# Eight row buffers and a new clearing in a Flamingo kernel's first feed-forward stage, and a second stage that routes a pair of blocks ahead

## The reference

```python
# layer 0: shared expert of width 8*128 plus 8 routed experts of width 4*128, two per token, each expert takes at
# most CAPACITY = 1.25 * 3200 / 8 = 500 tokens; the rest are dropped for it
y = (silu(x @ sg) * (x @ su)) @ sd
p = softmax(rms(x) @ router_w.T); top 2 of 8; weights p_k / (p_1 + p_2)
y += sum_k weight_k * (silu(x @ rg[e_k]) * (x @ ru[e_k])) @ rd[e_k]      # where the token's place in e_k < CAPACITY
# layer 1: shared expert of width 128 plus 32 routed experts of width 64, four per token
p = softmax(x @ gw + gb)
group score = sum of the best 2 of each group of 4 experts; keep the 4 best of 8 groups; top 4 experts of the kept
y = shared(x) + sum_k p_k * expert_k(x)                                    # silu(x@w1+b1) * (x@w3+b3) @ w2 + b2
```

## Time and profile before

| | us |
|---|---|
| median of 3 runs (lowest, highest) | 6456.21 (6451.88, 6462.94) |
| the profiled execution's own time | 6469.54 |
| its span, first to last instruction | 6467.7 |
| first feed-forward stage, from and to | 1387.3, 1811.2 |
| of it the 64 dense tiles, from | 1403.4 |
| of it the 32 expert tiles, from | 1610.8 |
| second feed-forward stage, from and to | 3624.9, 4134.9 |
| third feed-forward stage (unchanged), about, from and to | 4530, 4950 |

### The profile page before, as it was taken

How to read it: one execution, slowest core, us unless ns; L and a number is a source line. 1 busy time by engine, 2 the same in 40 slices (tenths; PEclk the granted TensorE clock), 3 DMA queues, 4 the chain that set the end, 5 groups by cost and what they waited for, 6 DMA issues and landing times. The chain is left out here.

```text
span 6467.7 us, 117098 instructions
## 1 busy us (share of the span) xinstructions
PE 5589.6 (86%) x40832; PEld 3686.0 (57%) x40832; DVE 4453.7 (69%) x12146; ACT 3253.6 (50%) x4807; POOL 1778.2 (27%) x1263
## 2 busy tenths in 40 slices
PE   6999999978559999999999566687496999999996
PEld 4666666647435555555555355455496566665663
DVE  6777777756356666666666577544676877788775
ACT  3666666644324444444444343333354566666664
POOL 2222222204122222222222023344364222222220
PEclk9999999988769999999999778788798999999998
DMA  3333333321133333333332133266232332333320
GB/s 78 74 72 73 74 74 74 75 63 34 38 94 78 78 78 78 78 78 78 77 76 66 42 64 62 68 192 170 91 111 81 74 73 66 71 70 75 74 61 22
DMA packets 220512, 494.21 MB, mean 76 GB/s; under 512 B 35531, under 2 KB 154242, under 8 KB 219773
## 3 DMA queue, kind: packets, MB, share of 16 engines
q1 hardware_dynamic: 214341, 483.03, 30.8%
q0 software_dynamic: 5632, 4.23, 0.3%
HBM read 262.45 MB, written 12.97 MB: 43 GB/s over the span
## 5 line engine op out<-in xcount | busy, mean ns | idle before, releaser
L850 PE MATMUL a_max<-a_stack,a_qblk 96*100 96x482 f32 (+1 forms) x4608 | 2003.3, 455 | 115.5 <-DVE a_mx L671 35.9
L550 ACT ACTIVATE a_probs<-a_scores 128x800 f32<-128x800 f32 (+1 forms) x1536 | 1281.5, 838 | 1019.9 <-PE a_scores L867 657.0
L863 PE MATMUL a_scores<-a_qblk,a_stack 128*128 128x400 f32 (+1 forms) x4608 | 1379.1, 372 | 5.9 <-POOL a_qblk L455 2.9
L665 DVE CUSTOM_DVE_ANT_0 a_dump<-a_max,a_mqf 100x482 f32<-100x482 f32 (+1 forms) x1536 | 978.7, 657 | 426.6 <-PE a_max L850 395.4
L850 PEld LDWEIGHTS a_max<-a_stack,a_qblk 96*100 96x100 f32 x4608 | 767.5, 167 | 746.6 <-issue 207.2
L671 DVE CUSTOM_DVE_ANT_0 a_dump<-a_max,a_penq 100x482 f32<-100x482 f32 (+1 forms) x1536 | 956.3, 657 | 274.0 <-PE a_max L850 252.5
L657 DVE TENSOR_REDUCE a_mx<-a_max 100x1 f32<-100x482 f32 (+1 forms) x1536 | 941.9, 655 | 260.1 <-PE a_max L850 242.3
L879 PE MATMUL a_pv<-a_probs,a_v_aug 128*32 128x200 f32 x18432 | 1052.1, 340 | 3.4 <-ACT a_probs L548 2.1
L863 PEld LDWEIGHTS a_scores<-a_qblk,a_stack 128*128 128x128 f32 (+1 forms) x4608 | 840.3, 186 | 181.6 <-issue 52.6
L548 ACT ACTIVATE a_probs<-a_scores,a_kbias 128x800 f32<-128x800 f32 (+1 forms) x768 | 697.6, 926 | 409.4 <-PE a_scores L863 409.1
L431 POOL TENSOR_TENSOR a_klo<-a_kf,a_khi 128x1444 fp32r<-128x1444 f32 x96 | 316.4, 3296 | 1507.8 <-ACT a_khi L511 1062.9
(11 more groups left out here) (390 smaller groups left out, 7314.5 us busy)
## 6 DMA issues: line engine op xcount, KB each, us to landing
a_stack<-a_khi SPq DMA_DIRECT2D x768, 180.5 KB, 3.4
a_ctxT<-in_ctxT_dram SPq DMA_DIRECT2D x128, 722.0 KB, 8.3
a_stack<-a_klo SPq DMA_DIRECT2D x384, 180.5 KB, 3.6
f_wb<-weights_by_token SPq DMA_DIRECT2D x16, 1600.0 KB
f_wb<-weights_by_token SPq DMA_DIRECT2D x64, 400.0 KB
a_ctxn<-in_ctxn_dram SPq DMA_DIRECT2D x32, 704.0 KB
a_mt_i<-in_mask1T_dram SPq DMA_DIRECT2D x32, 600.0 KB, 6.9
a_mq_i<-in_mask_dram SPq DMA_DIRECT2D x32, 564.1 KB
```

Of the source, the lines that this page charges most:

```text
L550: act.activation(out_, in_, ACT.Exp, scale=scale).then_inc(sc_free, 1)
L665: nc.vector.tensor_tensor_reduce(dump[:, k % 2, 0:n], src, mqf[:, b % 2, o:o + n], 1.0, -3.0e38, ALU.mult, ALU.max, out_).then_inc(mx_free, 1)
L850: pe.matmul(to[0:S, 0:n], qblk[0:96, b % 2, HALF * h + head, :], stack[0:96, b % 2, g, o:o + n], start=True, stop=True).then_inc(mx_full, 1)
L863: ins = pe.matmul(out_, stack[:, b % 2, 2 * h + g, kt * D:kt * D + r], qblk[:, b % 2, HALF * h + 4 * g:HALF * h + 4 * g + 4, :].rearrange( ...
```

## The change

In the first stage `got` has eight buffers instead of three, and SP issues all eight row fetches one after the other as soon as the scatters have landed, ahead of the weight parts of experts 3 to 7. `rows_by_slot` is cleared from 80 partitions (50 rows each, 528 B pieces as before), `rows_by_token` in pieces of 1024 floats (4 KB) out of a zeroed stretch at the end of `rows`. POOL's number fills of `sent` and DVE's normalising of the last block wait for the clearing, since they write there.

The second stage gets a function of its own, `grouped_ffn_phase`, without a hardware loop. The routing is made for two blocks at a time and one pair ahead, all x splits of the 8 blocks have buffers, group and expert choice use DVE's max and match_replace instructions, and the weight parts come in a new order.

```diff
-    LOADS = 2
+    BLANKS = 80
...
-        blank = sb("blank", [SLOT, ROW])
-        zero = sb("zero", [S, D])
-        got = sb("got", [SLOT, 3, 4, ROW])
+        blank = sb("blank", [BLANKS, ROW])
+        zero = rows[:, (B - BLK) * 2 * ROW:(B - BLK) * 2 * ROW + QB * D]
+        got = sb("got", [SLOT, E, 4, ROW])
...
-            sp.dma_start(rows_by_slot.rearrange("(a p) r -> p a r", p=SLOT), bc(blank[:, :], 1, 4 * E)).then_inc(inited, 16)
+            sp.dma_start(rows_by_slot.rearrange("(a p) r -> p a r", p=BLANKS),
+                         bc(blank[:, :], 1, E * CAPACITY // BLANKS)).then_inc(inited, 16)
             sp.wait_ge(blank_made, 2)
             for k in range(2):
-                sp.dma_start(rows_by_token[k].rearrange("(s b) d -> s b d", b=B), bc(zero[:, :], 1, B)).then_inc(inited, 16)
+                sp.dma_start(rows_by_token[k].rearrange("(s q b) d -> s q (b d)", q=QUARTERS, b=QB),
+                             bc(zero, 1, QUARTERS)).then_inc(inited, 16)
...
-            for e in range(3):
-                slots_load(e)
-            for e in range(AHEAD, E):
-                for half in range(per):
-                    part_load(shared_parts + per * e + half)
-                slots_load(e)
+            for e in range(E):
+                sp.dma_start(got[:, e, :, :],
+                             rows_by_slot[e * CAPACITY:(e + 1) * CAPACITY].rearrange("(j p) r -> p j r", p=SLOT)
+                             ).then_inc(got_in[e], 16)
+            for p in range(shared_parts + per * AHEAD, PARTS):
+                part_load(p)
...
+            pool.wait_ge(inited, 48)
             for k in range(2):
                 pool.iota(sent[:, :, k, D + 1:ROW].bitcast(U32), [[1, B], [0, ROW - D - 1]], base=B * S * k,
...
             def normalise(n):
+                if n == NBLK - 1:
+                    dve.wait_ge(inited, 48)
```

The new function's order of work (its tile is the same as before; QB = 8 sequences, a pair of blocks):

```diff
+        xh, xl = sb("xh", [D, NBLK, TOK], F32R), sb("xl", [D, NBLK, TOK], F32R)
+        wb = sb("wb", [D, 2, ROUTED, TOK])
...
+        for n in range(2, NBLK):
+            at = 2 * C * (n // 2 - 1) + 4 * (n % 2)
+            xn_at[at] = n
+            turn_at[at + 1] = n
+            split_at[at + 2] = n
+            logits_at[at + 3] = n
+            low_at[at + 3] = n
...
+        for p in range(1, PAIRS):
+            at = 2 * C * (p - 1)
+            shift_at[at + 8] = p
+            expo_at[at + 9] = p
+            score_at[at + 10] = p
+            keep_at[at + 12] = p
+            top_at[at + 14] = p
+            weight_at[at + 16] = p
+            w_turn_at[at + 18] = 2 * p
+            wT_at[at + 19] = 2 * p
+            w_turn_at[at + 23] = 2 * p + 1
+            wT_at[at + 24] = 2 * p + 1
+        EARLY = 3
+        part_at = {PART * (p - EARLY) + 1: p for p in range(EARLY, len(PARTS))}
...
+            part_load(0)
+            part_load(1)
...
+            weights_spread(0)
+            part_load(2)
+            weights_spread(1)
+            for p in range(3, len(PARTS)):
+                part_load(p)
+            for n in range(2, NBLK):
+                weights_spread(n)
...
+            def keep_groups():
+                for b in range(QB):
+                    mark(nc.vector.max(top[:, b, :], score[:, b, 0:8]))
+                settle()
+                step(nc.vector.memset(top[:, :, 4:8], ABSENT))
+                for b in range(QB):
+                    mark(nc.vector.match_replace(score_hit[:, b, :], top[:, b, :], score[:, b, :], HIT))
+                settle()
+                step(nc.vector.tensor_scalar(bound[:, :, :], score_hit[:, :, 0:8], HIT, 3.0, ALU.is_equal, ALU.mult))
+                step(nc.vector.scalar_tensor_tensor(kept[:, :, 0:E].rearrange("p b (g k) -> p b g k", k=4), bc(bound[:, :, :], 3, 4), -1.0,
+                                                    prob[:, :, :].rearrange("p b (g k) -> p b g k", k=4), ALU.add, ALU.min))
+
+            def top_experts():
+                for b in range(QB):
+                    mark(nc.vector.max(top[:, b, :], kept[:, b, 0:E]))
+                settle()
+                step(nc.vector.memset(top[:, :, 4:8], ABSENT))
+
+            def weights_of(p):
+                for b in range(QB):
+                    mark(nc.vector.match_replace(kept_hit[:, b, :], top[:, b, :], kept[:, b, :], HIT))
...
+            weights_of(0)
+            split_weights(0)
+            split_weights(1)
+            split_weights(2)
+            dve.wait_ge(weights_in, 64)
+            for g in range(TILES):
...
+                if g in part_at:
+                    split_weights(part_at[g])
+                if g >= SPLIT_LAG:
+                    hidden_low(g - SPLIT_LAG)
+                hidden(g)
```

More of the change, by code:

```diff
@@ L1639, in dispatched_ffn_phase @@
         sent_in = sem("sent_in")
-        got_in = [sem(f"got_in{i}") for i in range(3)]
+        got_in = [sem(f"got_in{i}") for i in range(E)]
         gu_ready, silu_ready, h_ready, down_done = sem("gu_ready"), sem("silu_ready"), sem("h_ready"), sem("down_done")
@@ L2729, in flamingo_kernel @@
             attention_phase(nc, "a1", x, xnT, ident, w, dram, D ** -0.5, gates[0:S, 1:2], mask=(A["mask1"], A["mask1T"]))
[L2730 removed]
+        w = {k: A[f"f1_{k}"] for k in ("wg", "wu", "wd", "router", "bg", "bu", "bd", "bshared", "brouter")}
+        grouped_ffn_phase(nc, "f1", x, ident, w, gates[0:S, 5:6], scratch)
         with nc.sbuf_tensor("xnT_a2", [D, B * S], F32) as xnT:
```

390 lines of the change are left out of this document (372 added, 18 removed).

## The result

The changed kernel takes **6189.34 us** (median, 6185.28 to 6199.85) where the kernel before takes 6459.57 (6451.88 to 6477.56) in the same comparison: ratio 0.958, 95% interval 0.9557 to 0.9604, or 270 us less. Forecast were 6199 us and 257.5 us less. The profiled execution took 6189.05 us, its span is 6187.3, the mean clock 0.946 for 0.930. Measured again beside other kernels (e5_again), the ratio was 0.959 (0.956 to 0.9619).

The account below looks back on a forecast made before the run. First stage bound by clearing and expert-row waits, second by routing and weight transfer, not by an engine. -20 - 88 + 5 - 154.5 = -257.5 us, giving 6199 us against the median; range 6150 to 6262.

Parts of the forecast that it names:

- part 1: First stage: clearing slot rows from 80 partitions and token rows in 4 KB pieces, -20 us (bounds 3 and 25.46).
- part 2: Expert part of the first stage: eight row buffers, an expert every 9.25 us, -88 us (bounds 93 and 74).
- code arrival: First stage's experts: code arriving late as 20 more scatters run beside work, +5 us (0 to 15).
- (b): Second stage's start: GpSimd's first multiply 22.1 us after the weights' store, then another 20 us until weight part 3 at tile 1.
- (c): Second stage, block 0: tiles 1 to 11 paced by weight parts, 19 us; six more tiles with routing, 14 us.
- (d): Second stage, seven blocks after the first: 227 us plus 14 for routing bursts, 241 us (bounds 227 and 257).
- (e): Second stage, from the last tile to the end: 7.5 us, as before the change.
- part 3: Whole second stage, with pairs routed ahead: ends at 3980.5 against 4134.9, -154.5 us.
- Rival 1: Whole kernel: no burst shows, no code wait, the whole clearing wait goes; 6175 us, chance 0.17.
- Rival 2: Second stage: spread weights late, half of 13.5 us per block stays in seven blocks; +47, 6246 us, chance 0.13.
- Rival 3: First stage's experts: their weights pace them at 12 us each; +14, 6213 us, chance 0.03.
- Rivals 4 and 5: Second stage: unrolled code late, +92, 6291 us, chance 0.10; or such waits behind spread transfers, four per block, 6485, 0.02.

Follow-up runs that it names:

- e5_again: The changed kernel measured and traced once more, code unchanged, on another chip: 6194.91 us, ratio 0.959 to the kernel before.
- e4_tokens80: The changed kernel with token rows cleared from 80 partitions instead of 100: 6208.73 us, ratio 0.9584 to the kernel before.
- e8_twice: The changed kernel with VectorE's piece that keeps the four best groups done twice in a row: 6207.89 us, ratio 0.9617 to the kernel before.
- e11_split: The changed kernel with two of VectorE's routing bursts cut in two, second halves one tile later: 6223.55 us, ratio 0.9602 to the kernel before.

## Why the prediction was right, and where not

**Forecast and measured by step**, in us, the second stage from its first transfer:

| step | forecast | measured |
|---|---|---|
| part 1, clearing | -20 | -12.8 |
| part 2, experts | -88 | -88.1 |
| part 2, code arrival | +5 | not seen |
| (a) first weights stored | 30.4 | 27.3 |
| (b) part 3 there, tile 1 goes on | 74.1 | 69.7 |
| (c) tile 11; block 0 ends | 93; 107 (last tile) | 97.2; 115.6 (result) |
| (d) seven blocks | 241 | 231.0 |
| (e) to the end | 7.5 (from the last tile) | 2.5 (from the result) |
| part 3 in all | -154.5 | -160.8 |

**Sum.** -12.8 - 88.1 - 160.8 = -261.7 us, against 261.1 by the three kernels with one part each, 262.4 in e5_again and 270.2 in the first comparison; no step accounts for the 8 us between these last two. The predicted 6199 lies 10 us over the median, 0.16%, less than a measurement can tell. The likeliest case came true. That the total is this close is partly luck: part 1 was 7 us too good, part 3 6 us too poor, and the +5 that did not come made up the rest.

**Part 1** was mis-sized. The rates came as I had them or better (slots 238 GB/s on all engines for my 205; tokens 250 in the stretch shown). By them the clearing takes 8.9 + 13.1 = 22.0 us for 40.6, 18.6 less. But I let the load behind the clearing gain 3 us too, and it lost 6: from 1390.81 to ScalarE's use at 1424.13 it is 33.3 us, 11.3 more than the clearing, where it was 5.5 before. The engines' share is 0.22 and then 0.14 in its last 6 us. How I read that: the load has its part on the engines that the tokens fill and lands last there. The views give only the mean share of the engines; that the wait falls by 3 to 5 us when the tokens use all of them (e4_tokens80) speaks for it. By the Trainium skill's rule on the number of engines (DMA: Bandwidth & Descriptors, "Why a DMA increments its semaphore by 16 and not by 1") I had estimated 7.7 us for the slots, which stands against 2.11 MB / 238 GB/s = 8.9 us; the sum by it, 22 to 23 us, fell with mine, for the same reason. "Under 6 us of wait" was wrong: 12.67.

**Part 2** came to a tenth of a microsecond, in the change and alone. The +5 had no ground: the row that it was taken from shows stalls that other traces of near variants, on other chips, have not, and no run shows that late code makes them.

**Part 3.** The step that I least trusted, the new stand at tile 1 for part 3, came at 69.7 us for 74 (by its own terms, 3677.4 and 20, the sum should have said 72.5). (c) was too short: tiles 1 to 11 took 27.6 us, not 19. VectorE has the splits of the weight parts, the turned blocks' splits and the first burst in them; from 3570 us to the end of block 0 it is busy 39.58 of 44 us, at a clock of 0.89:

```profile
3570.00:3614.00 44.00, 38.46 (x184) 34.20 (x184) 39.58 (x120) 27.58 (x58) 21.61 (x17) 0.89 0.11 33
```

```profile
3572.35 1.27 DVE L2453 TENSOR_TENSOR f_wg_lo<-f_whole,f_wg_hi 128x256 fp32r<-128x256 f32 x1
```

Three of its splits of weights take 1.27, 1.28 and 1.17 us for the 0.42, 0.42 and 0.28 of their like, each beside a GpSimd multiply: 2.6 us that my step had not, 1.7 of them in tiles 1 to 11. The rest of the 8.6 us no run divides.

(d) was too long: unrouted blocks took 30.9, 30.6 and 29.4 us for my 31, and a routed pair 70.0 for 74. The price of the bursts was right in kind (added length costs at least its length, e8_twice) and high in size: of four pieces only the scores open a gap of over 0.8 us, 2.90 before a weight load. My price had no term for the clock, which fell behind that gap. The ends of (c) and (e) are counted from different points; together they are 114.6 forecast and 118.1 measured.

**Rivals.** Rival 1 came near by its number but not by its reason: the clearing wait stayed. Rival 2 is refuted by the absence of any wait of GpSimd behind block 0. Rival 3 is refuted: experts come 9.25 us apart (46.25 / 5). Rivals 4 and 5 are too: no "remote" row in the second stage. That GpSimd's multiply would hold VectorE's two-input routing steps up and cost 20 to 25 us is refuted for this schedule: in a routed block one such step takes 0.80 us for 0.42 and one 0.59 for 0.42. The effect is there all the same, in e11_split, in the three splits of weights above, and in each tile's own split (f_hl from f_hb and f_hh, 0.57 us alone): 0.78 us in the mean of the routed block, 0.72 in the next one, with single ones at 1.40. Of that the forecast had a part in its price of a tile, taken from the third stage, where this split takes 0.67 in the mean.

## What to carry to other kernels

Before speeding up a transfer that something waits for, look at what stands behind it in the queue: moving two loads ahead of the token clearing gave 12 us, where the clearing at nearly twice the rate had given 13, and dealing a 3.2 MB transfer out in pieces between the loads gave 27 more. Take a burst's price from where it stands (what shares its tiles, which engine runs beside it), not from its length alone, and look at the clock behind it. In e11_split the halves in the next tile cost what they had saved. A wait that no engine and no transfer of the core releases should be seen in a second trace, on another chip, before any gain or loss is built on it.

## What was not expected of the hardware

- The dense part of one and the same code took 121 us or 139 to 146 us, mostly by chip or hour, with 13 to 31 us of ScalarE's waits marked "remote" in the second case. The kernel before takes some 25 us more in the comparisons that show it; the ratios hardly differ.
- Clearing from 80 partitions instead of 100 raised the share of the transfer engines from 0.69 to 0.98, but the rate only from 250 to 275 GB/s.
- A two-input instruction of VectorE of 0.42 us took 1.27 when it began 0.06 us after a GpSimd multiply of 1.05.
- After TensorE had stood 2.56 us in a routed block, its granted clock was 0.50 from 3668 to 3670 us; doing a VectorE piece twice there cost the block 2.8 us, and TensorE was busy 1.7 us longer for the same matmuls.
